# Turning the gathered expert tokens in blocks of 32 on VectorE and sending the blocks by sixteen transfers, instead of two TensorE transposes, in a fused attention and mixture-of-experts kernel

## What is computed

```
q, k, v = xn @ Wq.T + bq, xn @ Wk.T + bk, xn @ Wv.T + bv        # 16 heads of 64, keys of one batch
attention = softmax(q @ k.T / 8) @ v @ Wo.T + bo
probs = softmax(xn @ router_w.T); 8 of 64 experts per token, weights normed to sum 1
each expert takes its first 128 tokens: y = (silu(t @ w_gate) * (t @ w_up)) @ w_down   # F = 192
moe = sum of y * weight per token + shared expert of width 192 (silu(xn @ sg) * (xn @ su)) @ ws_down
```

## Time and profile before

| | us |
|---|---|
| median of 3 runs | 3419.74 (3418.6 to 3422.72) |
| profiled execution, time | 3419.81 |
| profiled execution, span | 3418.1 |
| TensorE busy | 3380.4 (99%) |
| VectorE busy | 2515.9 (74%) |
| GpSimd busy | 2798.8 (82%) |
| ScalarE busy | 1658.3 (49%) |

### The profile page before, as it was taken

One profiled execution on the slowest core, in us unless ns is written; L12 is line 12 of the kernel. 1 busy time (PEld: TensorE's weight loads), 2 busy tenths in 40 slices (PEclk: granted clock), 3 DMA queues, 4 the chain that ended last, 5 costly groups with the idle time before them and its releaser, 6 DMA issues.

```text
span 3418.1 us, 61564 instructions
## 1 busy us (share of the span) xinstructions
PE 3380.4 (99%) x16960; PEld 2076.6 (61%) x16960; DVE 2515.9 (74%) x3228; ACT 1658.3 (49%) x3175; POOL 2798.8 (82%) x2381
## 2 busy tenths in 40 slices
PE   8999899999999999999999999999999999999999
PEld 6888555555555555555555555555555555555599
DVE  8999677777777777777777777777777777777776
ACT  5666444444444444444444444444444444444543
POOL 3443499999999999999999999999999999999722
PEclk9999999999999999999999999999999999999999
DMA  7987656777677666667777767776767777766497
GB/s 220 279 257 244 175 145 179 190 186 182 188 184 189 185 184 184 183 182 194 190 185 186 185 183 186 188 183 184 183 179 191 190 187 186 184 186 168 135 354 252
DMA packets 424498, 666.27 MB, mean 195 GB/s; under 512 B 67456, under 2 KB 229120, under 8 KB 424448
## 3 DMA queue, kind: packets, MB, share of 16 engines
q1 hardware_dynamic: 410112, 644.68, 68.0%
q0 software_dynamic: 14336, 20.98, 3.4%
HBM read 305.01 MB, written 125.08 MB: 126 GB/s over the span
## 4 chain that ended last, share of the span: by engine, by line
PE 86%; DVE 1%; POOL 1%; issue 0%; ACT 0%; SPq 0%; DMA 0%; POOLq 0%; DVEq 0%
PE psum L1031 26%; PE psum L988 15%; PE psum L991 14%; PE psum L1092 11%; PE psum L1016 10%; PE psum L1199 5%; PE psum L1077 2%; PE psum L1046 2%; PE psum L1083 1%; PE psum L1084 1%; POOL sums L1634 0%; PE psum L1069 0%; POOL sums L1633 0%; DVE q_rest L1506 0%; DVE merged L1370 0%
## 5 line engine op out<-in xcount | busy, mean ns | idle before, releaser
L1289 ACT ACTIVATE probs<-psum 128x512 f32<-128x512 f32 x2048 | 1077.6, 603 | 1192.5 <-PE psum L991 1185.8
L1370 DVE TENSOR_REDUCE merged<-psum 128x1 fp32r<-128x1024 f32 x1024 | 1201.7, 1215 | 592.0 <-PE psum L1016 571.8
L1633 POOL TENSOR_TENSOR sums<-sums,probs 128x512 f32<-128x512 f32 x761 | 975.3, 1282 | 60.0 <-ACT probs L1289 1.8
L1634 POOL TENSOR_TENSOR sums<-sums,probs 128x512 f32<-128x512 f32 x761 | 976.2, 1283 | 0.0
L1031 PE MATMUL psum<-probs,v_sb 128*64 128x512 f32 x4096 | 935.1, 598 | 0.0
L988 PE MATMUL psum<-q_full,k_full 128*128 128x512 f32 x2048 | 860.9, 420 | 2.5 <-DVE merged L1370 1.6
L991 PE MATMUL psum<-q_rest,k_rest 65*128 65x512 f32 x2048 | 811.0, 396 | 0.0
L1031 PEld LDWEIGHTS psum<-probs,v_sb 128*64 128x64 f32 x4096 | 271.3, 136 | 562.1 <-issue 504.0
L988 PEld LDWEIGHTS psum<-q_full,k_full 128*128 128x128 f32 x2048 | 387.3, 189 | 178.9 <-issue 76.5
L991 PEld LDWEIGHTS psum<-q_rest,k_rest 65*128 65x128 f32 x2048 | 389.2, 190 | 67.2
L1092 PE MATMUL psum<-x_t,w_qk 128*128 128x512 f32 x1536 | 404.7, 399 | 0.7 <-PEq L1941 0.7
(11 more groups left out here) (164 smaller groups left out, 3385.0 us busy)
## 6 DMA issues: line engine op xcount, KB each, us to landing
x_t<-xt SPq DMA_DIRECT2D x118, 1024.0 KB, 6.9
k_full<-high SPq DMA_DIRECT2D x256, 256.0 KB
v<-values SPq DMA_DIRECT2D x64, 512.0 KB, 3.4
w_qk<-wqk_parts SPq DMA_DIRECT2D x64, 512.0 KB
v_sb<-v SPq DMA_DIRECT2D x64, 512.0 KB, 5.4
q_full<-high SPq DMA_DIRECT2D x128, 256.0 KB
q_full<-low SPq DMA_DIRECT2D x128, 256.0 KB
k_rest<-low SPq DMA_DIRECT2D x128, 256.0 KB
```

The source lines that it names most:

```text
L1289: nc.scalar.activation(probs[:, kt, h, :], score_bank(j), ACT.Exp, scale=SCALE).then_inc(probs_ready, 1)
L1370: nc.vector.tensor_reduce(out=merged[:, q // GROUP, col:col + 1], in_=work[:, 2 * h:2 * h + 2, :].rearrange("p b c -> p (b c)"), axis=AX, ...
L1633: nc.gpsimd.tensor_tensor(total[:, 0, :], first[:, 0, :], probs[:, kt, 0, :], ALU.add)
L1634: nc.gpsimd.tensor_tensor(total[:, 1, :], first[:, 1, :], probs[:, kt, 1, :], ALU.add).then_inc(sums_added, 1)
```

## The change

Gathered tokens: VectorE turns them in 32x32 blocks (`turn_tokens`, two instructions of 128x128, in group 3 of the step before, behind `reduce(s, 6)`), and SyncE moves block (b, m) to block (m, b) by sixteen transfers of 32 partitions and 256 bytes each (`turn_out`), at the end of its step, and so ahead of the next step's `place`. TensorE's two transposes and ScalarE's copy are gone; GU waits for the sixteen transfers.

Other parts: in PJ TensorE's wait for the reduction stands behind the waits for the loaded tokens and weights. In the head ScalarE writes the whole of each projection beside its high part (into `sums0`, free there) and GpSimd subtracts, in place of eight low parts on VectorE; the projections of pair 0 come in the order 1, 3, 0, 2; `place_first` brings pair 0 in two halves. In units 0 and 1 of the norm stage ScalarE does the router's exponential of the next unit later, behind the copies of the second hidden part. In the last step the first load of the output stage stands ahead of `spread_out(63)`.

```diff
-ITEMS = ({2: "PJ", 4: "XT"}, {2: "PJ", 4: "GU"}, {2: "PJ"}, {2: "PJ", 4: "DN"})
-HAS_ITEM = {"PJ": 3, "XT": 1, "GU": 1, "DN": 1}
+ITEMS = ({2: "PJ"}, {2: "PJ", 4: "GU"}, {2: "PJ"}, {2: "PJ", 4: "DN"})
+HAS_ITEM = {"PJ": 3, "GU": 1, "DN": 1}
...
-           ((), ("RAW0",), ()))
+           ((), ("RAW0",), ("XTURN",)))
...
+FIRST = (1, 3, 0, 2)
...
+    x_turn = sb("x_turn", [P, TURNS, KD, BLOCK])
+    x_et = sb("x_et", [P, TURNS, KD, BLOCK])
...
-                if nxt and not known(reduced - 1, 1):
-                    pe.wait_ge(quad_reduced, reduced - 1)
                 if which == 0:
                     pe.wait_ge(x_loaded[half], DMA * x_loads(s + 2))
                 if g == 0:
                     pe.wait_ge(w_loaded, 2 * DMA * (s + 3))
+                if nxt and not known(reduced - 1, 1):
+                    pe.wait_ge(quad_reduced, reduced - 1)
                 product(out, par, which, half)
-            elif name == "XT":
-                pe.wait_ge(quad_reduced, at_most(reduced - 1, QUADS * NP))
-                pe.wait_ge(tokens_loaded, DMA * (s + 1))
-                for kd in range(KD):
-                    last = nc.tensor.transpose(work[:, 1, kd * P:(kd + 1) * P], x_e[:, par, kd * P:(kd + 1) * P], ident[:])
-                last.then_inc(xt_filled, 1)
             elif name == "GU":
                 pe.wait_ge(quad_reduced, at_most(reduced - 1, QUADS * NP))
-                pe.wait_ge(xt_copied, s + 1)
+                pe.wait_ge(turns_landed, DMA * TURNS * TURNS * (s + 1))
...
-                                                x_et[:, kd, :], start=(kd == 0), stop=(kd == KD - 1))
+                                                x_et[:, :, kd, :], start=(kd == 0), stop=(kd == KD - 1))
...
+        def turn_tokens(p, par):
+
+            dve.wait_ge(tokens_loaded, DMA * (p + 1))
+            if not known(p, 1):
+                dve.wait_ge(turns_landed, DMA * TURNS * TURNS * p)
+            for k in range(KD):
+                last = nc.vector.transpose(x_turn[:, :, k, :], x_e[:, par, k * P:(k + 1) * P])
+            last.then_inc(x_turned, 1)
...
+        def low_of(s, n):
+
+            g = FIRST[n] if s == -2 else n
+            which, half = g % 2, g // 2
+            cols = slice(half * HALF, (half + 1) * HALF)
+            pool.wait_ge(full_ready, 4 * (s + 2) + n + 1)
+            nc.gpsimd.tensor_tensor(low[:, s % 2, which, cols], full(n), f32(high[:, s % 2, which, cols]),
+                                    ALU.subtract).then_inc(lows_ready, 1)
...
+        def turn_out(p):
+
+            waits = [(x_turned, p + 1)]
+            if not known(p, 1):
+                waits += [(turns_landed, DMA * TURNS * TURNS * p), (gu_filled, p)]
+            alone(sp, (standing, 1), *waits)
+            for b in range(TURNS):
+                for m in range(TURNS):
+                    sp.dma_start(x_et[BLOCK * m:BLOCK * (m + 1), b], x_turn[BLOCK * b:BLOCK * (b + 1), m]
+                                 ).then_inc(turns_landed, DMA)
...
+            if is_step(s, 0):
+                shift_out(s, par, 1)
+                turn_out(0)
             if nxt:
                 waits = [(lows_ready, 4 * (s + 2))]
...
                 alone(sp, (standing, 1), (lows_ready, 4 * (s + 2) + 4), (x_loaded[1], DMA * x_loads(s + 2)))
                 load_tokens(sp, io, keep, s + 3, 1)
+            if nxt:
+                turn_out(s + 1)
```

More of the change, by code:

```diff
@@ L435, in unit @@
                 values_out(5, 7)
-            if more:
+            if more and not known(u, 2):
                 router_exp(u + 1)
@@ L440, in unit @@
             nc.scalar.copy(hid1[0:F2, :], hidden1[:]).then_inc(hid_high, 1)
+            if more and known(u, 2):
+                router_exp(u + 1)
             if not more:
@@ L1134, in head @@
             pe.wait_ge(w_loaded, 2 * 2 * DMA)
-            for g in range(SLOTS):
+            for g in FIRST:
                 if g == 2:
@@ L1231, in item @@
                 which, half = g % 2, g // 2
-                if g == 0 and not known(s, 0):
-                    act.wait_ge(placed, DMA * SHUFFLES * (s + 1))
+                if g == 0 and is_step(s, 0):
+                    for n in range(2):
+                        act.wait_ge(first_placed[n], DMA * HALF_PLACED[n])
+                elif g == 0:
+                    act.wait_ge(placed, DMA * SHUFFLES * s)
                 act.wait_ge(pj_filled, 4 * (s + 2) + g + 1)
@@ L1466, in step @@
                     reduce(s, 2 * g)
+                if is_step(s, 0) and g == 0:
+                    turn_tokens(0, 0)
                 for name in FILLERS[g][2]:
@@ L1566, in head @@
                                     ).then_inc(earlier_ready, 1)
-            for g in range(SLOTS):
-                low_part(-2, 0, g, psum[:, g, :])
             for q in range(GROUP):
@@ L1706, in store, with place_keys @@
                          ).then_inc(out_stored[half], DMA)
-        def place_keys(pp):
+        def place_keys(pp, done):
             for h in range(2):
@@ L1711, in place_keys, with place_first, place @@
                     sp.dma_start(f32(k_full[to, pp, h, :]), f32(high[DK * h:DK * (h + 1), pp, 1, :])
-                                 ).then_inc(placed, DMA)
-        def place(pp, keys=True):
-            if keys:
-                place_keys(pp)
+                                 ).then_inc(done, DMA)
+        def place_first(half):
+            cols = slice(half * HALF, (half + 1) * HALF)
+            for h in range(2):
+                head_rows = slice(DK * h, DK * (h + 1))
+                if half == 0:
+                    sp.dma_start(f32(k_rest[0:DK, 0, h, :]), f32(low[head_rows, 0, 1, :])).then_inc(first_placed[0], DMA)
+                for dst, to, src in ((q_full[:, 0, h, cols], slice(0, DK), high), (q_full[:, 0, h, cols], slice(DK, P), low),
+                                     (q_rest[:, 0, half, h, :], slice(0, DK), high)):
+                    sp.dma_start(f32(dst[to]), f32(src[head_rows, 0, 0, cols])).then_inc(first_placed[half], DMA)
+        def place(pp):
+            place_keys(pp, placed)
             for h in range(2):
@@ L1749, in head @@
             sp.wait_ge(lows_ready, 4)
-            place(0, False)
+            place_first(0)
             shift_out(0, 0, 0)
+            place_first(1)
             sp.wait_ge(pj_filled, 4)
@@ L1771, in step @@
                 place(pp)
-            if att:
+            if att and not is_step(s, 0):
                 shift_out(s, par, 1)
```

117 lines of the change are left out of this document (68 added, 49 removed).

## The result

The changed kernel takes 4183.31 us (median; 4181.84 to 4192.67), the kernel before 3420.64 us beside it: 1.2236 times as long, 95% interval 1.2218 to 1.2254. The profiled execution has a span of 4180.9 us. The forecast was 4150 us, the range 3905 to 4290.

A forecast was written before the change was run, and what follows sets the result against it. TensorE, busy 99%, was taken to set the pace, with SyncE's queue becoming late: 3419.8 + 601 (62 steps, 9.7 us each) + 130 (lower clock behind waits) + 0 (ends) = 4151, rounded 4150 us; range 3905 to 4290.

The forecast's parts named there:

- What bounds it, and the place of the loss: TensorE sets the pace; sixteen transfers ahead of `place` on SyncE's queue make TensorE wait at group 2 and quad 4.
- The turns: VectorE's two 128x128 turns behind quad 6 take 0.9 us together, bounds 0.4 to 1.7.
- The transfers: SyncE's sixteen transfers ahead of `place` take 16 x 0.63 = 10.1 us, bounds 6.1 to 13.4.
- What stands behind `place`: `place` starts 13.7 us later, and everything behind it on SyncE's queue, `shift_out` and `spread_out`, moves with it.
- The slack of 4.0 us: `place` can start 4.0 us later before TensorE waits: 3.2 ahead of NORM0, 0.8 more behind it.
- low part at 1080.72, done by 1081.38: VectorE's group 2 low part behind NORM0, wanted by quad 4 at 1082.22, gives 0.8 us more slack.
- The clock: TensorE runs at a lower clock behind its waits: 2.1 us a step, bounds nothing and 2.9, 130 us in all.
- a loss behind the first wait: TensorE waits 4 to 5 us for `shift_out` at group 2; clock loss behind it goes into quad 4's wait.
- The sum: 3419.8 + 601 (62 steps, 9.7 us each) + 130 of clock + 0 at the ends = 4151, rounded 4150 us.
- the ends: Lead-in and output: gain of at most 5 us against expert 0's tokens in step 0; 0, bounds -8 to +8.
- Rival 2: Transfers fit in if out of the way by `place` plus 4.0 us of slack: faster, about 3395; chance 0.05.
- the transposes: TensorE's two transposes removed: 0.22 us a step, 14 us over 64 steps, if TensorE still sets the pace.

The follow-up runs named there:

- The doses: Kernel before with 16, 10 or 6 idle 32-partition, 8 KB transfers ahead of `place` on SyncE's queue, nothing turned: 3950.82, 3839.27 and 3512.53 us.
- spread_first: Changed kernel with only `spread_out` moved forward, past the next expert's weights and the next pair's values: 3832.30 us.
- early_spread: early_turn with `spread_out` moved ahead of the next expert's weights and the next pair's values: 3417.12 us, 0.9993 of before.
- extra6: Kernel before with six idle transfers of 32 partitions and 8 KB issued ahead of `place`: 3512.53 us.
- early_turn: Changed kernel with the turns behind NORM1 and the sixteen transfers between the second store and the second half of the input tokens: 3740.48 us.
- extra16: Kernel before with sixteen idle transfers of 32 partitions and 8 KB issued ahead of `place`: 3950.82 us.
- early_ends: early_spread with expert 0's tokens turned ahead of step 0's first low part and step 62's output bias loads moved later: 3406.37 us, 0.9960 of before.
- early: Changed kernel with turns behind NORM1, the sixteen transfers ahead of the second store, that store behind `place`, the input-token load behind `spread_out`: 3952.95 us.
- extra10: Kernel before with ten idle transfers of 32 partitions and 8 KB issued ahead of `place`: 3839.27 us.
- rest_alone: Changed kernel with its token part undone, all the rest of the change kept: 3405.02 us, 0.9952 of before.

## Why the prediction was right, point by point

- **What bounds it, and the place of the loss: right.** The sixteen transfers ahead of `place`, the waits at group 2 (62 times) and at quad 4 (61 times) stand in the profile as named. The doses show that transfers alone do it, spread_first that the way through `spread_out` ended last, early_spread that neither the turns nor the transfers cost a step anything where the order gives them room.
- **The turns: 0.9 us taken, 0.49 measured**, and nothing waited for them but the transfers. The difference moved the sum by 0.4 us a step. By the figure of the Trainium skill (VectorE: DVE Perf Modes, The three transpose paths), 311 ns each, it would have been 0.62, an estimate; this trace shows 0.245 each, in four-byte numbers.
- **The transfers: 10.1 us taken, 10.11 measured.** `place` was to start 13.8 us behind the start of quad 6's reductions (1063.4 - 1049.56) and started 13.2 behind it (1063.72 - 1050.53).
- **What stands behind `place`: 13.7 us late taken, 12.0 measured** at `spread_out`. `place` started 13.2 us late in the median step and ran 12.0 us instead of 13.5. The prediction had this only in its range.
- **The slack of 4.0 us: 2.7 + 0.7 measured**, by the means of the 50 steps. In the changed kernel the end of `spread_out` is 11.9 us late and NORM0 9.2 late, which leaves 2.7 ahead of NORM0, where I had 3.2: with nothing to spare NORM0 starts 1.9 us behind that end, where I had 1.4. Behind NORM0 the slack is 0.7, where I had 0.8; extra6 agrees, where steps grow once NORM0 is about 1 us late.
- **The step that failed, though it didn't show: "low part at 1080.72, done by 1081.38" as a fixed distance from NORM0.** NORM0 and SILU0 took 2.5 us in the mean instead of 0.98. So quad 4 is 11.9 - 2.7 - 0.7 + 1.5 = 10.0 us late, against 9.7 forecast. By luck the errors met: 1.8 us too much lateness (13.7 for 11.9) on one side, 0.6 us too much slack and 1.5 of growth left out on the other.
- **The clock: 2.1 us a step taken, 2.2 measured** behind quad 4. The number was a choice between bounds, and the reason given for it (a longer wait holds more of the slow stretch) isn't borne out: early_turn, whose waits at quad 4 are 3.6 us in the mean (201.2 us in 56), loses 2.0 behind them, and extra16, with 6.0 us (366.1 in 61), 2.2. That a loss behind the first wait goes into the second was right: with the second wait mostly gone (spread_first) the first becomes the bound.
- **The sum.** 62 x (10.0 + 2.2) = 756 us instead of 731; the remaining 7 of the 763 measured are at the ends, which I had put at 0 with bounds of 8: step 0 starts 3.8 us sooner and is 5.8 us longer (GU waits for expert 0's tokens), step 62 grew by 3.4 us more than the others, and the output by 1.9 (distances between the reductions of quad 7 in both traces).
- **Rivals.** Rival 2 (faster because they fit in) named the right point: the transfers must be out of the way by `place` plus its slack, unless the order behind `place` changes. In early_turn `place` starts 4.3 us late and just misses that point; in early_spread it starts 5.2 us late, and the pace is kept only because `spread_out` was moved as well. early_ends reaches 3406 and not 3395: the transposes were worth less than I had taken (below), and step 0 is longer.
- **The expectations that missed** by their time: early, spread_first and early_spread for the reasons told with them. The others (extra6, extra10, early_turn) all had the mistakes that the prediction had without harm: the slack is 3.4 us and not 4.0, and beyond it I counted no growth on VectorE; extra6 and early_turn put little or nothing for the clock as well. In early_turn NORM0 is 2.3 us late, 1.3 to 1.6 beyond the edge, and the step 5.3 us longer.

What is read from traces and was not tried by itself: that it is GpSimd's additions that stretch NORM0 and SILU0. No run took GpSimd away, but the twelve traces together leave little room for another cause. They hold 768 SILU0: of the 302 that began while an addition into `sums` was running, 297 took more than 0.4 us (median 1.35); of the 466 others none took more than 0.36. Lateness alone doesn't do it: extra16's NORM0 is 6.7 us late, its SILU0 meets no addition, and all 64 are short:

```profile
L1427 DVE TENSOR_SCALAR silu_e<-silu_e x64: 251/286/294, 412.2 to 3730.3; 128x256 f32<-128x256 f32 x64
```

## What to carry to other kernels

Price a block of transfers by their number on the issuing queue, times what like transfers take there, and then follow what stands behind it on that queue to the first consumer that has no slack; sending the same block earlier, and putting short urgent transfers ahead of loads that have room, was worth 766 us here (early_spread against the changed kernel). Lateness beyond the slack is not paid one for one: past the edge a late instruction may fall beside another engine's work and grow, and here TensorE paid some 2 us in the clock behind each such wait, whether it was 3.6 us long in the mean or 6.0. So keep well inside the edge rather than at it.

## What the runs showed that was not expected

- **VectorE's NORM0 and SILU0 beside GpSimd's additions.** SILU0 takes 0.29 us alone and 1.35 beside them, NORM0 0.69 and up to 1.8. SILU0 (ns, min/median/max) in the changed kernel, and, in the fence behind it, in spread_first:

```profile
L1453 DVE TENSOR_SCALAR silu_e<-silu_e x64: 253/1347/1360, 414.0 to 3962.7; 128x256 f32<-128x256 f32 x64
```

```profile
L1453 DVE TENSOR_SCALAR silu_e<-silu_e x64: 251/289/1385, 414.4 to 3610.9; 128x256 f32<-128x256 f32 x64
```

  The Trainium skill (SBUF — State Buffer, Who interferes with whom) says that a VectorE instruction with two SBUF inputs contends with a GpSimd instruction that reads SBUF, that a `tensor_scalar` can do so in a two-port mode, and that in such a mode whichever of the two issues later is held up until the first is through. The traces agree, as far as they go: NORM0 has two SBUF inputs, SILU0 is a `tensor_scalar`, and the 28 SILU0 that were already running when an addition began took no more than 0.29 us; in which mode SILU0 ran, no row shows.
- **Two kinds of steps in one run.** extra6 has steps of 44.5 and of 46 to 50.5 us in the same execution, and its four times spread over 55 us where those of early and early_turn lie within 20: it stands on the edge.
- **The transposes' worth.** Between the products they took 0.22 us a step; the median step of rest_alone is 44.34 us and that of early_ends, without them, 44.30. Some four fifths of the gain went elsewhere; in both kernels TensorE's weight loads still wait for exponentials and reductions now and then. What takes up the gain was not tried, and the two kernels differ in the order on the queue as well.
